# First attention of an eight-stage kernel: value tiles padded to 32 columns, score products over 32 rows, exponentials over two PSUM banks, maxima over one, head 0 loaded by itself

## What is computed

```python
def _L0_attn_ref(x, Wqkv, bqkv, Wo, bo):      # HEADS = 16, hd = 8
    qkv = x @ Wqkv.T + bqkv
    qkv = qkv.reshape(B, H, S, 3 * hd)
    q, k, v = jnp.split(qkv, 3, axis=-1)
    scores = jnp.einsum('bhsd,bhtd->bhst', q, k) * (1.0 / math.sqrt(hd))
    attn = jax.nn.softmax(scores, axis=-1)
    vals = jnp.einsum('bhst,bhtd->bhsd', attn, v)
    vals = vals.reshape(B, S, D)
    return vals @ Wo.T + bo
...
x = x + _L0_attn_ref(_layernorm(x, axis=-1), ...)
```

## Time and profile before

| | |
|---|---|
| runs of the kernel | 3782.70, 3783.51, 3792.18 us |
| median | 3783.51 us |
| profiled execution, its own time | 3783.76 us |
| its span, first to last instruction | 3782.0 us |
| around the span | 1.8 us |
| first attention, PE from first maximum to last output | 49 to 1272 us of the span |

### The profile page before, as it was taken

The page is one execution under the profiler, slowest core; times in us unless marked ns, Lnnn a source line. Parts: engine busy times, 40 slices in busy tenths (PEclk is TensorE's granted clock), DMA queues, the critical chain, the costliest instruction groups (busy, mean ns, idle before and its releaser), DMA issues. The chain is left out here.

```text
span 3782.0 us, 40627 instructions
## 1 busy us (share of the span) xinstructions
PE 3351.0 (89%) x14344; PEld 1691.4 (45%) x14344; DVE 2344.3 (62%) x4243; ACT 1438.6 (38%) x2536; POOL 797.2 (21%) x621
## 2 busy tenths in 40 slices
PE   5999999999999879999999999999999756566799
PEld 2333333333333445555555555555554332344577
DVE  4555555555555157777777777777774567666554
ACT  1444444444444314444444444444444221100253
POOL 0000000000000014444444444444444000144100
PEclk6555555555555579999999999999999858555599
DMA  4111111111110041111111111111110000000000
GB/s 89 11 11 12 22 12 11 15 18 12 11 11 1 7 101 23 34 29 33 34 29 29 31 30 34 34 34 34 34 34 1 11 6 2 0 1 1 28 1 12
DMA packets 71887, 83.96 MB, mean 22 GB/s; under 512 B 26358, under 2 KB 61868, under 8 KB 65196
## 3 DMA queue, kind: packets, MB, share of 16 engines
q1 hardware_dynamic: 71684, 81.36, 11.5%
HBM read 25.10 MB, written 5.24 MB: 8 GB/s over the span
## 5 line engine op out<-in xcount | busy, mean ns | idle before, releaser
L428 DVE TENSOR_REDUCE l0s_mpair<-l0s_mx 128x1 f32<-128x1024 f32 x512 | 626.9, 1224 | 520.9 <-PE l0s_mx L309 486.3
L914 ACT ACTIVATE l1a_PT<-l1a_st 128x512 f32<-128x512 f32 x1024 | 604.8, 598 | 876.7 <-PE l1a_st L823 869.9
L931 DVE TENSOR_REDUCE l1a_m<-l1a_aux 128x1 f32<-128x512 f32 x1024 | 673.4, 686 | 186.9 <-PE l1a_aux L786 171.6
L408 ACT ACTIVATE l0s_PT<-l0s_st 128x512 f32<-128x512 f32 x1024 | 534.0, 597 | 642.3 <-PE l0s_st L328 642.3
L882 POOL TENSOR_TENSOR l1a_acc<-l1a_acc,l1a_PT 128x1024 f32<-128x1024 f32 x224 | 556.3, 2483 | 715.3 <-ACT l1a_PT L914 715.3
L328 PE MATMUL l0s_st<-l0s_QS,l0s_KS 25*128 25x512 f32 x1024 | 531.8, 753 | 4.2 <-ACT l0s_PT L408 4.2
L345 PE MATMUL l0s_ov<-l0s_PT,l0s_V 128*9 128x512 f32 x2048 | 485.1, 1040 | 39.1 <-ACT l0s_osb L395 35.5
L836 PE MATMUL l1a_ov<-l1a_PT,l1a_V 128*64 128x512 f32 x2048 | 512.1, 622 | 0.0
L821 PE MATMUL l1a_st<-l1a_QA,l1a_KA 128*128 128x512 f32 x1024 | 451.1, 441 | 2.4 <-issue 2.3
L823 PE MATMUL l1a_st<-l1a_QB,l1a_KB 65*128 65x512 f32 x1024 | 413.5, 404 | 0.0
L786 PE MATMUL l1a_aux<-l1a_KA,l1a_QA 128*128 128x512 f32 x1024 | 404.6, 437 | 6.9 <-DMA l1a_QA<-l1a_lo 5.4
(11 more groups left out here) (348 smaller groups left out, 3147.7 us busy)
## 6 DMA issues: line engine op xcount, KB each, us to landing
l1a_KA<-l1a_hi SPq DMA_DIRECT2D x32, 512.0 KB, 7.5
l0s_QS<-qk_parts SPq DMA_DIRECT2D x192, 64.0 KB
l1a_QA<-l1a_hi SPq DMA_DIRECT2D x16, 512.0 KB, 4.6
l1a_QA<-l1a_lo SPq DMA_DIRECT2D x16, 512.0 KB, 4.2
l1a_QB<-l1a_hi SPq DMA_DIRECT2D x16, 512.0 KB, 4.6
l1a_KB<-l1a_lo SPq DMA_DIRECT2D x16, 512.0 KB, 6.5
l0s_KS<-qk_parts SPq DMA_DIRECT2D x192, 16.0 KB
l3f_w<-in_L_ffn_w SPq DMA_DIRECT2D x3, 792.0 KB
```

The lines of the kernel that those rows point to most:

```text
L408: nc.scalar.activation(PT[:, g % PT0, e, :], st[:, b % ST0, :], ACT.Exp).then_inc(exp_done, 1)
L428: nc.vector.tensor_reduce(mpair[:, u % 2, tile, pair:pair + 1], mx[:, n % MX0, :, :].rearrange("p e k -> p (e k)"), axis=AX.X, op=ALU.max) ...
L914: nc.scalar.activation(PT[:, g % PT_SLOTS, (u % 2) * CW:(u % 2 + 1) * CW], st[:, u % ST1, :], ACT.Exp).then_inc(exp_done, 1)
L931: nc.vector.tensor_reduce(m4[:, b, q, c:c + 1], src, axis=AX.X, op=ALU.max).then_inc(aux_read, 1)
```

## The change

- `values` uses 32 columns of `V` instead of 9 (8 values, a one, 23 zeros); the clearing of `ov` goes away. `scores` uses rows 24 to 31 too: the maximum, and seven rows in which `QS` is zero.
- `V`, `QS` and `KS` are set in the first stage, while x loads (`V` on POOL, the other two on DVE), and live for the whole attention.
- `st` has 2 slots of two banks; both scores of a step share one slot, and ACT takes one exponential of 1024 columns for them. PE waits for the exponential of two steps before.
- `mx` has 3 slots of one bank. Each of the two maxima of a step is a task with a slot and a DVE reduction of 512 columns; four maxima for each query tile are joined (`mquad`).
- The value projections go to steps 16 to 19 instead of before step 0 and to 2, 4 and 6.
- The first 128 tokens of q and k are placed alone, and head 0 is loaded before the other tokens are placed.

```diff
-BUF0, MX0, ST0, PT0 = 3, 2, 3, 6
+BUF0, MX0, ST0, PT0 = 3, 3, 2, 6
...
-    mx = ps("mx", [P, MX0, 2, CW])
-    st = ps("st", [P, ST0, CW])
+    mx = ps("mx", [P, MX0, CW])
+    st = ps("st", [P, ST0, 2, CW])
...
+        if LEAD0 - 5 <= g < LEAD0 - 1:
+            out.append(("v", g - LEAD0 + 5))
         if g < ALL:
-            out.append(("max", g))
-        if g in (2, 4, 6):
-            out.append(("v", g // 2))
+            out += [("max", 2 * g), ("max", 2 * g + 1)]
...
-                    for e in range(2):
-                        r = slice(32 * (2 * pair + e), 32 * (2 * pair + e) + R0)
-                        q = QS[r, h % BUF0, half * HALF0:(half + 1) * HALF0].rearrange("r (k i) -> r i k", i=TILES0)
-                        last = nc.tensor.matmul(o[:, e, :], q[:, tile, :], KS[r, h % BUF0, :], start=True, stop=True)
+                    r = slice(32 * (2 * pair + e), 32 * (2 * pair + e) + R0)
+                    q = QS[r, h % BUF0, half * HALF0:(half + 1) * HALF0].rearrange("r (k i) -> r i k", i=TILES0)
+                    last = nc.tensor.matmul(o, q[:, tile, :], KS[r, h % BUF0, :], start=True, stop=True)
...
+                if g >= ST0:
+                    pe.wait_ge(exp_done, g - ST0 + 1)
                 for e in range(2):
-                    b = 2 * g + e
-                    if b >= ST0:
-                        pe.wait_ge(exp_done, b - ST0 + 1)
-                    r = slice(32 * (2 * pair + e), 32 * (2 * pair + e) + R0 + 1)
+                    r = slice(32 * (2 * pair + e), 32 * (2 * pair + e) + 32)
                     at = half * HALF0 + qc * CW
-                    nc.tensor.matmul(st[:, b % ST0, :], KS[r, h % BUF0, a * P:(a + 1) * P], QS[r, h % BUF0, at:at + CW],
-                                     start=True, stop=True).then_inc(st_full, 1)
+                    last = nc.tensor.matmul(st[:, g % ST0, e, :], KS[r, h % BUF0, a * P:(a + 1) * P],
+                                            QS[r, h % BUF0, at:at + CW], start=True, stop=True)
+                last.then_inc(st_full, 1)
...
-                        last = nc.tensor.matmul(ov[col:col + HD0 + 1, :], V[:, u // 2, KPG0 * (2 * pair + e) + a, :],
+                        last = nc.tensor.matmul(ov[col:col + 32, :], V[:, u // 2, KPG0 * (2 * pair + e) + a, :],
...
-                for e in range(2):
-                    b = 2 * g + e
-                    act.wait_ge(st_full, b + 1)
-                    nc.scalar.activation(PT[:, g % PT0, e, :], st[:, b % ST0, :], ACT.Exp).then_inc(exp_done, 1)
+                act.wait_ge(st_full, g + 1)
+                nc.scalar.activation(PT[:, g % PT0, :, :], st[:, g % ST0, :, :], ACT.Exp).then_inc(exp_done, 1)
...
-                    nc.vector.tensor_reduce(mpair[:, u % 2, tile, pair:pair + 1],
-                                            mx[:, n % MX0, :, :].rearrange("p e k -> p (e k)"),
+                    nc.vector.tensor_reduce(mquad[:, u % 2, tile, 2 * pair + e:2 * pair + e + 1], mx[:, n % MX0, :],
                                             axis=AX.X, op=ALU.max).then_inc(reduced, 1)
...
-            place(0)
-            place(1)
+            place(0, slice(0, P))
             load(0)
-            place(2)
-            place(3)
+            place(0, slice(P, CW))
             load(1)
+            place(1, slice(CW, 2 * CW))
             load(2)
+            place(2, slice(2 * CW, 3 * CW))
+            place(3, slice(3 * CW, 4 * CW))
```

More of the change, by code:

```diff
@@ L180, with l0_attention @@
 J0 = D // HD0
-def l0_attention(nc, W, norm, X, xnT, ident, ones):
+def l0_attention(nc, W, norm, X, xnT, ident, ones, V, QS, KS):
     with ExitStack() as ctx:
@@ L187, in l0_attention @@
         with ExitStack() as actx:
-            used = l0_attend(nc, actx, W, norm, xnT, vals, ones)
+            used = l0_attend(nc, actx, W, norm, xnT, vals, ones, V, QS, KS)
         with ExitStack() as octx:
@@ L248, in l0_attend @@
     bias_scaled, full_done, rounded, split = sem("bias_scaled"), sem("full_done"), sem("rounded"), sem("split")
-    parts_out = [sem(f"parts_out{c}") for c in range(NC)]
+    parts_out = {t: sem(f"parts_out{t}") for t in (0, 1, TPC, 2 * TPC, 3 * TPC)}
     heads_in = [sem(f"heads_in{i}") for i in range(BUF0)]
-    ks_set, v_set, v_done, ov_zeroed = sem("ks_set"), sem("v_set"), sem("v_done"), sem("ov_zeroed")
+    v_done = sem("v_done")
     reduced, m_done, m_placed = sem("reduced"), sem("m_done"), [sem(f"m_placed{i}") for i in range(2)]
@@ L277, in tasks_of @@
         return out
-    plan = [[("qk", c) for c in range(NC)] + [("v", 0)]] + [tasks_of(g) for g in range(END)]
+    plan = [[("qk", i) for i in range(2 * NC)]] + [tasks_of(g) for g in range(END)]
     slot = {key: n for n, key in enumerate(key for tasks in plan for key in tasks)}
@@ L289, in mx_task @@
                     pe.wait_ge(mx_free[n % MX0], n // MX0)
-                o = mx[:, n % MX0, :, :]
+                o = mx[:, n % MX0, :]
                 if kind == "qk":
-                    for j in range(2):
-                        last = nc.tensor.matmul(o[:, j, :], Wt[:, j, :], xnT[:, i * CW:(i + 1) * CW],
-                                                start=True, stop=True)
+                    c, j = divmod(i, 2)
+                    last = nc.tensor.matmul(o, Wt[:, j, :], xnT[:, c * CW:(c + 1) * CW], start=True, stop=True)
                 elif kind == "v":
@@ L369, in fill @@
             def fill(c):
-                n = slot[("qk", c)]
-                act.wait_ge(mx_full, n + 1)
                 if c >= 2:
                     act.wait_ge(split, c - 1)
[L374 to L379, removed]
+                for j in range(2):
+                    n = slot[("qk", 2 * c + j)]
+                    act.wait_ge(mx_full, n + 1)
+                    if j == 0:
+                        nc.scalar.activation(full[:, c % 2, 0, :], mx[:, n % MX0, :], ACT.Identity,
+                                             bias=scaled_bias[:, :], scale=scale).then_inc(full_done, 1)
+                    else:
+                        nc.scalar.activation(full[:, c % 2, 1, :], mx[:, n % MX0, :], ACT.Identity,
+                                             bias=bias[:, 1:2]).then_inc(full_done, 1)
+                    act.wait_ge(full_done, 2 * c + j + 1)
+                    act.sem_inc(mx_free[n % MX0], 1)
                 nc.scalar.activation(hi[:, :, c * CW:(c + 1) * CW], full[:, c % 2, :, :], ACT.Copy).then_inc(rounded, 1)
@@ L415, in _ @@
         def _(dve):
-            nc.vector.memset(ov[:, :], 0.0).then_inc(ov_zeroed, 1)
             for c in range(NC):
@@ L448, in _, with place @@
                     ).then_inc(mx_free[n % MX0], 1)
-        @block.gpsimd
-        def _(pool):
-            nc.gpsimd.memset(KS[:, :, :].bitcast(F32), -1.0).then_inc(ks_set, 1)
-            nc.gpsimd.memset(V[:, :, :, :], 1.0).then_inc(v_set, 1)
         @block.sync
         def _(sp):
-            def place(c):
-                at = slice(c * CW, (c + 1) * CW)
-                sp.wait_ge(rounded, c + 1)
-                sp.dma_start(parts[0, :, :, at].rearrange("i p s -> p i s"), hi[:, :, at].bitcast(F32)
-                             ).then_inc(parts_out[c], 16)
+            def place(c, tokens):
                 sp.wait_ge(split, c + 1)
-                sp.dma_start(parts[1, :, :, at].rearrange("i p s -> p i s"), lo[:, :, at].bitcast(F32)
-                             ).then_inc(parts_out[c], 16)
+                for n, part in enumerate((hi, lo)):
+                    sp.dma_start(parts[n, :, :, tokens].rearrange("i p s -> p i s"), part[:, :, tokens].bitcast(F32)
+                                 ).then_inc(parts_out[tokens.start // P], 16)
             def load(h):
-                sp.wait_ge(parts_out[h // TPC], 32)
+                first = 0 if h == 0 else 1 if h < TPC else TPC * (h // TPC)
+                sp.wait_ge(parts_out[first], 32)
                 if h >= BUF0:
-                    sp.wait_ge(st_full, 4 * STEPS0 * (h - BUF0 + 1))
+                    sp.wait_ge(st_full, 2 * STEPS0 * (h - BUF0 + 1))
                 tokens = slice(h * P, (h + 1) * P)
@@ L2165, in program @@
         ones = sb("ones", [P, P])
-        load_stage(nc, x, X, ident, ones, (sem("x_loaded"), sem("ident_zero"), sem("consts_done")))
         W["loads"] = Loads(sem("weights_loaded"))
         norm_sems = norm_semaphores(sem)
+        load_sems = [sem(n) for n in ("x_loaded", "ident_zero", "consts_done", "v_zeroed")]
         for r, i in enumerate(range(8)):
@@ L2173, in program @@
             if i == 0:
-                l0_attention(nc, W, norm, X, xnT, ident, ones)
+                with ExitStack() as first:
+                    sb0, _, _ = stage_memory(nc, first, "l0")
+                    V = sb0("V", [P, H0, J0, 32])
+                    QS = sb0("QS", [P, BUF0, S], F32R)
+                    KS = sb0("KS", [P, BUF0, KPG0 * P], F32R)
+                    load_stage(nc, x, X, ident, ones, V, QS, KS, load_sems)
```

(1 more changed line is left out.)

52 lines of the change are left out of this document (27 added, 25 removed).

## The result

The changed kernel takes 3924.8 us (median of 4 runs, 3922.55 to 3927.14), beside 3786.0 us (4 runs, 3782.70 to 3792.18) for the kernel before: ratio 1.0365, 95% interval 1.0347 to 1.0383, 139 us slower. The profiled execution took 3927.1 us, with a span of 3925.4.

The account below looks back on a forecast made before the run. PE, at half clock in a fixed order with waits, bounds the kernel; the last score's start sets each quad. Terms +90.7, +34.8, +9.3, +4.9, +4 and -12 made +132 on 3783.8: 3916 us, 8-in-10 range 3795 to 3960.

Parts of the forecast that it names:

- 185 regular quads: PE's ordinary round of four maxima, four scores and values: from 4.14 to 4.63 us, +0.49 each, +90.7 us.
- padding: Wider value weights (9 to 32 columns) add 0.02 us a quad, +4.9 over 245; scores' extra rows add 0.
- 30 copy quads: Once a unit, values wait for ACT's copy behind the longer exponential: 5.49 to 6.65 us, +1.16 each, +34.8.
- 30 transposing quads: Once a unit, transposing products wait for maximum 2's slot: 6.58 to 6.89 us, +0.31 each, +9.3.
- start: Before the first score: first maximum 7 us earlier, 21 steps at DVE's pace +6.2, fourth value projection +4.6; +4 in all.
- tail: Last 10.5 quads, without maxima: no `ST0` wait, next quad at T+2.97 against 4.1; -12 us.
- bounds: Quads 46 to 118 and 30 to 55 us, start -3 to +14: total given as 3855 to 3968 us.
- Prices: Durations assumed for the rebuilt quad: 512-column reduction 0.687 us, 1024-column exponential 1.05, value projection 4.6.
- rival 1: PE's clock rises because padded value products fill all 128 columns: 3512 us, or anything up to 3780; chance 0.09.
- Rival 2: Fourth maximum doesn't wait, DVE freeing its slot in time: quad 3.4 us, up to -170, 3615 us; chance 0.07.
- 3: No difference: start, tail and quads cancel, quad +0.04 us at most; chance 0.03.

Follow-up runs that it names:

- Experiment 2: Changed kernel with each DVE reduction over 256 of the 512 columns, half of the keys left out of the maxima: 3851.9 us, ratio 1.0155.
- 1: Changed kernel with both scores of a quad's second step issued ahead of the fourth maximum: 3796.4 us, ratio 1.0013.
- 5: Kernel before with one-bank maxima alone, in four slots, reduced 512 columns at a time; exponentials stay single: 3784.5 us, ratio 0.9992.
- experiment 10: Changed kernel with the first 1024 tokens placed ahead of head 0's loads again, as in the kernel before: 3932.7 us, ratio 1.0386.
- experiment 11: Changed kernel, still padded, with the maxima of the odd key groups left out: 3605.0 us, ratio 0.9520.
- 12: Changed kernel with the odd key groups' maxima left out and without padding (values of 9 columns, scores over 25 rows): 3601.0 us, ratio 0.9510.
- 7: Changed kernel with PE order scores, values, maxima in each step and the copy behind the exponential of step 1: 3731.2 us, ratio 0.9839.
- 9: Kernel 7 with all four value projections ahead of the first maximum: 3717.7 us, ratio 0.9822.
- experiment 3: Changed kernel without the padding: values of 9 columns, scores over 25 rows, `ov` cleared first: 3919.7 us, ratio 1.0327.

## Why the prediction was right, and where it was off

The forecast was 3916 us by one mechanism, and the mechanism is shown: the fourth maximum waits for the slot of the first. It was forecast at T+1.66 and stands at T+1.65; the last score at T+2.26 and T+2.27; values at T+2.81 and T+2.83. Experiment 2 moves the wait by the reduction's length, 1 takes the scores out from behind it, 5 takes the slot reuse away, and each changes the quad as it should.

| term | forecast | measured | |
|---|---|---|---|
| 185 regular quads | +90.7, padding +3.7 | 185 x 0.54 = +100 | values 1.86, not 1.82 |
| 30 copy quads | +34.8, +0.6 | 30 x 1.03 = +31 | |
| 30 transposing quads | +9.3, +0.6 | 30 x 0.34 = +10 | |
| start | +4 | +9.4 (first score 91.8, 101.2) | loads not shorter |
| tail | -12 | -15.7 (last maximum to last values 48.1, 32.4) | clock |
| first attention | +132 | +134.1 (its last values start at 1268.9, 1403.0) | |

The total is nearer than its terms. With their padding, the regular quads came 5.5 us above the forecast and the copy quads 4.5 below it, the start 5.4 above and the tail 3.7 below. That 3 us are left of this together is partly luck. The bounds were also added up wrongly: as given they make 3850 to 3964, not 3855 to 3968, and 9 us for the loads gives a start of +3, not -3.

- **Prices.** Reduction 0.691 (0.687), exponential 1.02 (1.05), value projection (54.1 - 35.1)/4 = 4.75 (4.6), the norm stage 2.0 later (2). The padding was mis-sized: 0.04 a quad, 10 us, where I took 0.02 from the slope of the loads' durations. It lies between the first four value products and the second four, which follow after 0.85 instead of 0.82. The copy quad was forecast at 6.65 and took 6.51: the copy started 0.10 ahead of the end of the exponential (603.40 and 603.50), and I had it wait for the end.
- **The start is the step that failed.** I took 10 us for head 0's 24 loads. They took 18.4: SP needs 28.74 to 38.29 to issue them, and the last lands 8.8 later. That bound stood in the earlier trace rows as 19.7, and I laid it to the placements; experiment 10 puts these in front again, and the first maximum moves by 1 to 4 us only. First maximum 47.1, not 42, and so first score 101.2, not 95; the projections and DVE's pace behind it came as forecast.
- **The tail.** At half clock its shorter quads give -10 (unpadded: 37.9); the other 5.6 came with the clock at 1.00, which I had excluded. This is rival 1, for 17 of the stage's last 27 us; in the steady part it did not happen. The Trainium skill's rule in "TensorE: Matmul & The Clock Gate", Part 1 (the clock follows how busy PE has recently been) orders these rows no better than those before: in experiment 11, 94% busy stood at 0.50 and 75% at 1.00.
- **Rivals 2 and 3** fell with the trace: the fourth maximum waits. Rival 2's quad of 3.4 came in no kernel that takes all the maxima; the shortest are 4.15 with single exponentials and 4.26 with those over two banks.
- **The rest of the program**, whose code is unchanged, took 2508.5 us from the first product behind the attention before and 2519.1 after. In the twelve experiments it took 2514 to 2520, so the execution profiled before was shorter here than all of them. The largest piece is the last block; windows before, then after:

```profile
3565.80:3782.00 216.20, 200.47 (x1120) 151.75 (x1120) 102.22 (x264) 95.02 (x154) 11.71 (x3) 0.92 0.02 6
```

```profile
3704.40:3925.40 221.00, 205.12 (x1120) 155.00 (x1120) 101.99 (x264) 94.95 (x154) 11.68 (x3) 0.89 0.02 6
```

The same 1120 products take 4.8 us longer at a mean clock of 0.89 instead of 0.92. Where the clock rises in a later stage shifts with when the stage begins; that is argued from these rows, no run tested it. The 10.6 us of this unchanged code are most of what lies between 3916 and the profiled 3927.

## What to carry to other kernels

Splitting a buffer into smaller slots helps only if the slots are counted against the order on the engine that fills them: four tasks between two values and three slots mean that the fourth waits for the consumer of the first, and everything in order behind it waits too. Before giving a change up, look at what stands behind its wait: here putting the maxima last, and the copy two exponentials earlier, turned +3.7% into -1.6%, and 1.0% of that was to be had without the change. And head 0's load took as long as its issues on the queue (9.6 us) and the wait behind the last one (8.8); read both off the trace before promising that fewer bytes in front will shorten a load.

## What was not expected of the hardware

- PE at 1.2 GHz while 94% busy for 940 us, and at 2.4 GHz while 75% busy in the tail (windows of experiments 11 and 12). Nearly all that rose in this attention is tail, with scores and values alone; but the turned kernels (7 and 9) also have three short stretches each at 1.00 in their steady part, and the tails of the kernel before (40 us) and of experiment 3 (29 us) stayed at 0.50. What decides is open.
- Two scores on other row groups than a maximum that starts with them take 0.79 together; where one shares its row group, it starts 0.61 later and they take 1.24. In the turned kernel this is the 0.43 of 4.69 us by which its quad is shorter.
